# Attention and two-expert FFN on one core: rows of maxima and weight loads issued by ACT in place of SP

## What is computed

```python
x = x + _L0_xattn_ref(_layernorm(x, axis=-1), ctx_2048, ctx_2048, gamma)
    # qk = einsum('bhdq,bhdl->bhql') / 4;  softmax over l;  einsum('bhql,bhdl->bhdq')
x = x + _L0_ffn_ref(_layernorm(x, axis=-1), ...)
    # top = argmax(x Wg^T)
    # out0 = gelu(x W0a^T + b0a) W0b^T + b0b;  out1 = relu(x W1a^T + b1a) W1b^T + b1b
```

## Time and profile before

| | |
|---|---|
| median of 3 runs | 268.23 us (266.91 to 270.09) |
| the profiled execution's own time | 267.05 us |
| its span, first to last instruction | 264.8 us |
| PE busy | 228.1 us, 86% |
| DVE, ACT, POOL busy | 167.5, 134.7, 63.9 us |
| mean granted TensorE clock | 0.972 |
| issues by SP: stack copies, maxima rows | 87 and 30 |

### The profile page before, as it was taken

How to read it: one execution, slowest core, us unless ns; L and a number is a source line. 1 busy time by engine, 2 the same in 40 slices (tenths; PEclk the granted TensorE clock), 3 DMA queues, 4 the chain that set the end, 5 groups by cost and what they waited for, 6 DMA issues and landing times.

```text
span 264.8 us, 4862 instructions
## 1 busy us (share of the span) xinstructions
PE 228.1 (86%) x1858; PEld 172.2 (65%) x1872; DVE 167.5 (63%) x348; ACT 134.7 (51%) x208; POOL 63.9 (24%) x112
## 2 busy tenths in 40 slices
PE   0748947869599999999999999999999989989995
PEld 0425524444478676867686768676867676869893
DVE  3775687989635787578757875787476615333302
ACT  2014335665249454945494549554944494632230
POOL 6592120335700431043104310431101011011000
PEclk9999999798779999999999999999999999999999
DMA  4589999989712447375837582646202000000101
GB/s 158 85 156 165 207 289 171 253 165 153 102 22 80 101 136 110 100 107 123 116 101 102 125 117 62 99 97 108 64 0 64 0 22 2 20 22 0 40 2 40
DMA packets 19562, 25.75 MB, mean 97 GB/s; under 512 B 2644, under 2 KB 13140, under 8 KB 19284
## 3 DMA queue, kind: packets, MB, share of 16 engines
q1 hardware_dynamic: 18312, 24.25, 46.7%
q10 hardware_dynamic: 1228, 1.19, 2.1%
HBM read 11.28 MB, written 2.10 MB: 51 GB/s over the span
## 4 chain that ended last, share of the span: by engine, by line
PE 58%; ACT 17%; DVE 9%; DMA 7%; issue 7%; POOL 0%; SPq 0%; ACTq 0%; DVEq 0%
PE ff L740 21%; PE ff L723 12%; PE st L654 8%; DMA qkst<-mlow 6%; PE od L666 6%; ACT P L513 5%; ACT hid L542 4%; PE smax L642 3%; ACT L542 3%; PE st L629 2%; PE od L674 2%; ACT L513 2%; DVE nmax L351 2%; DVE y L423 1%; DVE yt L418 1%
## 5 line engine op out<-in xcount | busy, mean ns | idle before, releaser
L513 ACT ACTIVATE P<-st 128x1024 f32<-128x1024 f32 x64 | 65.8, 1028 | 85.4 <-PE st L654 76.9
L358 DVE TENSOR_REDUCE nmax<-smax 128x4 f32<-128x1024 f32 x54 | 66.2, 1226 | 40.2 <-PE smax L642 38.9
L740 PE MATMUL ff<-w2t,hid 128*128 128x256 f32 x256 | 60.0, 379 | 1.5 <-issue 1.1
L740 PEld LDWEIGHTS ff<-w2t,hid 128*128 128x128 f32 x256 | 47.7, 190 | 5.8
L723 PE MATMUL ff<-xnTh,w1h 128*128 128x256 f32 x128 | 39.1, 306 | 9.0 <-DVE y L423 3.4
L239 POOL TENSOR_TENSOR mv<-mv,power 128x1 f32<-128x1 f32 x31 | 18.3, 591 | 103.8 <-DVE mv L323 103.8
L654 PE MATMUL st<-qkst 50*128 50x256 f32 x240 | 31.2, 339 | 9.1 <-DMA qkst<-mlow 5.5
L723 PE MATMUL ff<-xnTl,w1h 128*128 128x256 f32 x128 | 37.1, 290 | 0.0
L723 PE MATMUL ff<-xnTh,w1l 128*128 128x256 f32 x128 | 37.1, 290 | 0.0
L654 PEld LDWEIGHTS st<-qkst 50*128 50x128 f32 x240 | 18.5, 191 | 26.2 <-issue 14.4
L666 PE MATMUL od<-P,vt 128*32 128x256 f32 x512 | 33.5, 406 | 0.0
(11 more groups left out here) (73 smaller groups left out, 250.9 us busy)
## 6 DMA issues: line engine op xcount, KB each, us to landing
qkst<-parts SPq DMA_DIRECT2D x87, 128.0 KB, 4.7
xv<-in_xv SPq DMA_DIRECT2D x16, 256.0 KB, 2.9
qk<-in_qk SPq DMA_DIRECT2D x15, 256.0 KB, 4.6
out<-y SPq DMA_DIRECT2D x16, 128.0 KB, 2.4
w1t<-in_w SPq DMA_DIRECT2D x1, 1024.0 KB, 10.2
w2t<-in_w SPq DMA_DIRECT2D x1, 1024.0 KB, 9.9
qkst<-parts ACTq DMA_DIRECT2D x3, 128.0 KB, 6.2
qk<-in_first SPq DMA_DIRECT2D x1, 256.0 KB, 3.4
```

The source lines that it names most:

```text
L358: dve.tensor_reduce(nmax[:, c % 2, :, :, j].rearrange("p a e -> p e a"), (ff if c in WIDE and j % 2 else smax)[:, :, :, :], AX.X, ALU.max, ...
L513: act.activation(P[:, b % 2, j, :, :, :].rearrange("p e a l -> p (e a l)"), st[:, :, :, :].rearrange("p e a l -> p (e a l)"), ACT.Exp, sca ...
L740: mm = pe.matmul(ff[:, t, u // HM, :], hid[:, u, t * C:(t + 1) * C], w2t[:, u, :], start=False, stop=u == UNITS - 1)
```

## The change

The helper `max_rows` moves from SP's program into ACT's. It is called at `k == 1`, which is `j == 2`: after `exp(b, 2)` and ahead of `copy_od(b-1)` (for b = 0, n = 2 after the exp of pair 3 of batch 0). ACT now waits for its own copy (`s_mhi`) and for DVE's (`s_mrow`) and issues the two 8 KB transfers. The two weight loads move to ACT too: `w1` at n = 0 behind the exp of pair 1 of batch 0, `w2` at n = 4 behind `exp(1, 0)`. SP keeps all else in its order. The transfers themselves and all arithmetic stay the same.

```diff
--- before.py
+++ after.py
@@ SP
-            def max_rows(c):
-                s = place(c, 4)
-                for n, part in enumerate((mhigh, mlow)):
-                    sp.wait_ge((s_mhi, s_mrow)[n], c)
-                    sp.dma_start(qkst[STACK + n:STACK + n + 65:64, s, :, 0, :].bitcast(F32),
-                                 part[:, c % 2, :].bitcast(F32)).then_inc(s_mst[s], 16)
...
-                if b + 1 < B:
-                    max_rows(b + 1)
                 if b + 2 < B:
                     load_xv(b + 2)
-                if b == 0:
-                    sp.dma_start(w1t[:, :, :, :].rearrange("p a e f -> p (a e f)"), w1).then_inc(s_w1, 16)
-                if b == 1:
-                    sp.dma_start(w2t[:, :, :].rearrange("p u l -> p (u l)"), w2).then_inc(s_w2, 16)
@@ ACT
+            def max_rows(c):
+                s = place(c, 4)
+                for n, part in enumerate((mhigh, mlow)):
+                    act.wait_ge((s_mhi, s_mrow)[n], c)
+                    act.dma_start(qkst[STACK + n:STACK + n + 65:64, s, :, 0, :].bitcast(F32),
+                                  part[:, c % 2, :].bitcast(F32)).then_inc(s_mst[s], 16)
...
+                if n == 0:
+                    act.dma_start(w1t[:, :, :, :].rearrange("p a e f -> p (a e f)"), w1).then_inc(s_w1, 16)
+                if n == PAIRS:
+                    act.dma_start(w2t[:, :, :].rearrange("p u l -> p (u l)"), w2).then_inc(s_w2, 16)
...
+                if k == 1 and 2 <= c <= B:
+                    max_rows(c - 1)
                 if j == 2 and b >= 1:
                     copy_od(b - 1)
```

## The result

The changed kernel takes 275.15 us (median of 4 runs, 274.38 to 275.79), the kernel before beside it 268.5. The ratio is 1.023, with a 95% interval of 1.019 to 1.027: slower by 2.3%, some 6 us. The forecast was 268.8 with a range of 265.0 to 273.5; it was wrong, and the time lies outside the range. Where an execution ran slowed by its clock, as e10's profiled one (378.68 us) and one of e14's (270.80) did, medians and ratios leave it out.

What follows compares the result with a forecast made beforehand. PE was taken to bound 72 to 206 us, with only 5.5 us of early row waits to gain. 267.05 - 0.4 + 0.3 + 0.9 = 267.85; on the runs' median 269.0, put at 268.8, range 265.0 to 273.5.

Steps and rivals of the forecast that it cites:

- What bounds the kernel: Whole kernel: PE sets the steady time; rows landing at once could save at most 5.5 us, all before 58 us.
- Latency on ACT's ring: Low row on ACT's ring under load: 2.8 us from issue to landing, between bounds of 1.9 and 5.4.
- step 1: First row: issued at 32.5, landed 1.0 us earlier; weight delays stack set 3 by 2.6 us, leaving -0.5.
- SP loses waits at L190; its next stack set waits for ACT's high part, as now, so nothing moves there either: SP's program, batches 0 to 3: removing its waits for the row shifts nothing there, no time charged.
- Rows 2 and 3: Rows issued at 43.85 and 54.15, landed at 46.65 and 56.95; total stays -0.5, then becomes -0.7.
- Step 4: Row 4, up to the first gemm1: ACT's issues start ods 0.3 us later; total at 70.67 is -0.4.
- The steady stage: Later batches: ACT's issues delay ods, costing 0.3 us over odd batches and 0.9 over even ones.
- Rival A: ACT issues wait until the datapath is empty, 1.2 us behind every exp(b,2): slower, 277 us, chance 0.10.
- Rival B: ACT's ring brings nothing, rows take 5.4 us in the first batches: slower, 275.4 us, chance 0.08.

Runs made afterwards that it cites:

- e10: Changed kernel plus 18 matmuls whose result nobody reads, on PE ahead of scores(1,0): 272.70 us, ratio 1.013.
- e14: e12 plus 8 unread matmuls ahead of scores(1,0) and 8 ahead of the first gemm1: 267.29 us, ratio 0.993.
- e8: Kernel before, all on SP, rows of batches 1 to 3 issued behind the loads of xv, weight and next qk: 274.05 us, ratio 1.016.
- e1: Changed kernel with the two weight loads back on SP, only the rows issued by ACT: 274.31 us, ratio 1.018.
- e6: e1 with SP waiting, in batches 0 to 3, for ACT's high part of batch b+4 before its loads: 270.22 us, ratio 1.002.
- e3: Changed kernel with the first weight issued on ACT behind the first pair of rows (n = 2): 275.18 us, ratio 1.019.
- e4: Changed kernel with the first weight issued on ACT ahead of its loop: 272.32 us, ratio 1.009.
- e12: Kernel before with the weights issued later on SP (b = 1, b = 3), first weight's high part at b = 3: 269.52 us, ratio 0.999.
- e13: Kernel before plus 8 unread matmuls ahead of scores(1,0) and 8 ahead of the first gemm1: 267.57 us, ratio 0.993.
- e15: e13 with 4 unread matmuls ahead of scores(1,0) and 5 ahead of the first gemm1: 267.25 us, ratio 0.992.

## Why the prediction was wrong, step by step

- **What bounds the kernel** was right: the steady stage had nothing to give, and the whole effect is before the first `gemm1`.
- **Latency on ACT's ring** is the step that failed. The text took 2.8 us for the first row, 1.9 plus eight packets' turns, and 8.3 were measured. The issue itself came as worked out: 33.11 is the 32.5 of step 1 and the 0.65 us by which this trace is late. Under load the row did not get its turn between SP's packets; e8 and e1 show the same landing from either ring. On quiet engines the small number is right: the second row, issued at 49.98 with the engines' share at 0.02 to 0.05, was there by 52.21, 2.2 us later. The fourth, issued at 71.97 while the engines were full, was used at 74.44, 1.4 us after they emptied (share 0.94 up to 73.0, then 0.12).
- **"SP loses waits at L190; its next stack set waits for ACT's high part, as now, so nothing moves there either"** is the sentence that hid it. The stack set did not move; the loads of `xv` and `qk` between them did, by 1.8 and 2.1 us, and so came in front of the row. I listed what was behind the wait and priced only the transfer that had a reader soon. e6, which puts that wait back in another form, removes the loss. Step 1 sized the weight's delay (2.6 us) only for stack set 3 and not for the row itself, although the row stands behind the same backlog; e1 against e3 and e4 gives this term 2.7 to 3.2 us.
- **Rows 2 and 3** were to be issued 2.2 to 2.9 us later and land 2.8 us after that. They were no longer waited for at all, since with PE 5 us late the engines had caught up: 8 GB/s between 50 and 52 us, where row 2 was issued (49.98) and used by 52.21.
- **Step 4**'s 0.3 us for `ods` and what follows was about right. In batch 3 of the changed kernel the issues start with the exp (71.06) and not ahead of it, and the second begins only at 71.97, 0.4 us after the first has ended; what holds it the trace doesn't show.

```profile
71.06 1.03 ACT L500 ACTIVATE P<-st 128x1024 f32<-128x1024 f32 x1 [3.53 <-PE st L654]
...
71.97 0.53 ACTq L519 DMA_DIRECT2D qkst<-mlow  x1
72.54 0.60 ACT L524 ACTIVATE ods<-od 128x512 f32<-128x512 f32 x1 [0.46 <-issue]
```

  `ods` starts 1.48 us behind the exp, where it started 0.92 behind it, and from that exp to the first `gemm1` it is 7.27 us (71.06 to 78.33) against 6.92 (63.75 to 70.67): 0.35 us of the 2.5 are the issues' cost on ACT.
- **The steady stage** was too dear: 0.3 + 0.9 us charged, nothing found. The covers (odd: `ods` just before the transpose) held as worked out. For even batches the range's lower end was the truth. The Trainium skill's account (Perfetto Trace Analysis, Per-engine timelines), by which the sequencer pushes an activation into a queue and goes on, agrees here: the issue at 167.15 lies 2.6 us ahead of the exp that precedes it in the program. Rival A, a drained datapath, is excluded by the same line.
- **Rival B** came nearest, with 275.4 against 275.15, and had a chance of 0.08. Its condition was met (a latency over 4.2 us), its mechanism too as far as that the ring brings nothing. But its sum is right by chance: it took 5.4 us for each of three rows, where one took 8.3 and the other two were not waited for. (By its own terms its third row would be +6.6 and not +6.4, as 54.15 + 4.2 + 5.4 is 63.75 against 57.13.) The Trainium skill's rule beside it (DMA: Bandwidth & Descriptors, Issuing engines are not separate DMA queues), that issuing from several engines saves only the sequencer's time, is borne out by e1 and e8 for this row. I had set against it the turns between rings of the same page of the Trainium skill (Queues, rings and completion order), which a large transfer does seem to get: with the weight on ACT and stack set 3 on SP the engines moved 206 to 360 GB/s from 31 to 35 us, against the 133 of the earlier trace rows. Why an 8 KB row doesn't, no run here shows.
- **PE's pace** was in no step. Between the two traces, the 2.5 us from `scores(1,0)` to the first `gemm1` come near what three value products add, 10.87 us against 8.38. That this is the path is not shown: the same products take 10.31 us in e12 and 10.21 in e6, and neither is measurably slower than before; and both traces of before are of executions with a mean granted clock of 0.972, where most of that kernel's have 0.966 to 0.968, e12's 0.967 and the changed kernel's four 0.967. No term for the pace was made, though the trace of before had the pattern: 0.80 us for four score matmuls at 36.26 and 0.50 at 46.67.

The windows behind the ring's turns, of the changed kernel (columns as in the earlier trace rows):

```profile
31.00:32.00 1.00, 1.00 (x8) 0.60 (x4) 0.96 (x4) 0.00 (x0) 0.00 (x0) 1.00 0.95 360
...
34.00:35.00 1.00, 0.00 (x0) 0.00 (x0) 1.00 (x3) 0.24 (x1) 0.00 (x0) 1.00 0.97 206
35.00:36.00 1.00, 0.00 (x0) 0.00 (x0) 1.00 (x2) 0.39 (x1) 0.54 (x1) 1.00 1.12 118
...
50.00:52.00 2.00, 1.36 (x12) 0.95 (x12) 1.94 (x5) 1.90 (x4) 0.00 (x0) 1.00 0.02 8
```

PE is idle from 34 to 41 us in them, and the load on the engines is what it waits behind.

Open: the 0.65 us at the start; why the row waits for the whole backlog and not for its turn; and how the 2.5 us, less the 0.35 of ACT's issues, divide between pace and queue, since the one trace that could have told, e10's, is of an execution with about half the clock, and no trace of before has the clock that most of its executions have.

## What to carry to other kernels

A wait in a DMA queue also holds back what is issued behind it. Before moving one to another engine, list every transfer it was holding, and ask which transfer will stand behind them: here loads that nobody needed soon, two of them in the changed kernel, ended up in front of an 8 KB row that PE was waiting for. A second ring didn't help a small transfer over a backlog; where a small one is urgent, issue the large ones after it, whichever engine issues.

## What the runs showed of the hardware

- From either of the two rings an 8 KB row landed only behind what was issued before it: 5.4 to 9.3 us from issue to use (e4, e3, e1, e8), in which the engines moved 1.0 to 2.3 MB. On quiet engines it took 2.2 us at most (changed kernel, 49.98 to 52.21).
- ACT's sequencer issues DMAs ahead of activations that stand before them in the program but still queue for the datapath: 2.6 us ahead at 167.15. An issue took 0.52 us and cost the datapath nothing there; in batch 3, where the issues began only with the exp (71.06), the activation behind them came 0.56 us later.
- PE ran the same 32 matmuls of the first batch in 1.93 (e13), 2.84 (before) or 3.64 us (changed), in windows whose granted clock read 1.00 each time. Matmuls whose result nobody reads, put into its waits, made the kernel 0.7 to 0.8% faster than before (e13, e14, e15).
